# A selective-scan kernel: the softplus chain in two halves with its PSUM copies on VectorE, and the forcing term by a product with a diagonal in some states

## What is computed

```python
xs = jax.nn.silu(xs)                      # 256 tokens x 512 channels
proj = xs @ xproj_w                       # 512 columns of dt, 64 of B, 64 of C
dt = jax.nn.softplus(proj[..., :512] + dt_bias)
def step(hst, ins):                       # over the tokens
    dA = jnp.exp(dt_t[:, :, None] * A)    # 64 states per channel
    hst = hst * dA + (dt_t * x_t)[:, :, None] * B_t[:, None, :]
    y_t = jnp.einsum('bds,bs->bd', hst, C_t)
y = ys + xs * Dskip
return y * jax.nn.silu(z) @ out_w
```

## Time and profile before

| | |
|---|---|
| median of 3 runs | 3404.33 us (3403.07 to 3409.16) |
| the profiled execution's own time | 3408.53 us |
| its span, first to last instruction | 3406.7 us |
| mean granted clock of PE | 0.947 of full speed |
| steady d = 0 pass (from 985.3 us) | 197.7 us |
| steady d = 1 pass (from 1183.0 us) | 207.1 us |
| last pass (d = 1, no side work; from 3181 us) | about 185 us |
| C rows from DRAM | 1024 DMAs of 128 KB, 2.9 us to landing |

### The profile page before, as it was taken

One profiled execution on the slowest core, in us unless ns is written; L12 is line 12 of the kernel. 1 busy time (PEld: TensorE's weight loads), 2 busy tenths in 40 slices (PEclk: granted clock), 3 DMA queues, 4 the chain that ended last, 5 costly groups with the idle time before them and its releaser, 6 DMA issues.

```text
span 3406.7 us, 69419 instructions
## 1 busy us (share of the span) xinstructions
PE 3024.2 (89%) x21944; PEld 2683.9 (79%) x21944; DVE 2909.5 (85%) x3331; ACT 2989.0 (88%) x6469; POOL 2945.7 (86%) x1552
## 2 busy tenths in 40 slices
PE   8778898999988999899988999899998899998776
PEld 6568787888878888788877888788887888887765
DVE  3269998899888998889988999889988899899885
ACT  1189999899989999899999999899998999999994
POOL 0069998999888998889988998889988899899995
PEclk6689999999989999899999999899998999999998
DMA  4011111111111111111111111112111111111210
GB/s 174 0 42 43 48 45 47 42 51 48 43 48 47 47 47 42 49 45 48 45 47 43 49 48 43 48 41 52 48 43 46 48 47 46 42 45 45 54 47 26
DMA packets 163033, 162.50 MB, mean 48 GB/s; under 512 B 17610, under 2 KB 156874, under 8 KB 162644
## 3 DMA queue, kind: packets, MB, share of 16 engines
q1 hardware_dynamic: 162644, 157.69, 17.2%
HBM read 154.44 MB, written 3.18 MB: 46 GB/s over the span
## 4 chain that ended last, share of the span: by engine, by line
PE 45%; POOL 16%; ACT 15%; issue 13%; DVE 9%; DMA 1%; DVEq 1%; POOLq 0%; ACTq 0%; SPq 0%
POOL hst L408 12%; PE ps L1225 12%; PE ps L1241 11%; ACT dA L567 7%; PE ps L993 6%; ACT uBT L553 4%; DVE hst L892 4%; PE ps L1002 4%; POOL uBT L417 4%; PE ps L1065 3%; PE ps L1040 2%; PE ps L1114 1%; PE ps L1049 1%; PE ps L1233 1%; PE ps L1150 1%
## 5 line engine op out<-in xcount | busy, mean ns | idle before, releaser
L408 POOL TENSOR_TENSOR hst<-hst,C_sb 128x1024 f32<-128x1024 f32 x1024 | 2441.0, 2409 | 232.8 <-DVE hst L892 226.6
L892 DVE TENSOR_TENSOR_SCAN hst<-dA,ps 128x512 f32<-128x512 f32 x2048 | 2384.0, 1205 | 177.6 <-PE ps L1241 160.1
L567 ACT ACTIVATE dA<-dt,A 128x255 f32<-128x255 f32 x4096 | 1758.5, 504 | 2.8 <-DVE hst L892 2.7
L1225 PE MATMUL ps<-ident,uBT 128*128 128x128 f32 x8192 | 1288.2, 281 | 134.0 <-DVE hst L892 103.0
L1241 PE MATMUL ps<-ident,hst 128*128 128x128 f32 x8192 | 1267.9, 278 | 104.5 <-POOL hst L408 103.7
L1225 PEld LDWEIGHTS ps<-ident,uBT 128*128 128x128 f32 x8192 | 994.2, 145 | 299.0 <-DVE hst L892 152.5
L553 ACT ACTIVATE uBT<-uT,BT 128x512 f32<-128x512 f32 x1536 | 1052.2, 720 | 130.9 <-PE ps L1225 120.0
L1241 PEld LDWEIGHTS ps<-ident,hst 128*128 128x128 f32 x8192 | 979.6, 144 | 139.8 <-POOL hst L408 139.7
L417 POOL TENSOR_TENSOR uBT<-uT,BT 128x512 f32<-128x512 f32 x512 | 559.3, 1092 | 185.3 <-DVE uT L829 185.3
L476 ACT ACTIVATE probs<-ps,nmax 128x128 f32<-128x128 f32 (+1 forms) x256 | 93.9, 423 | 101.6 <-DVE nmax L764 100.7
L993 PE MATMUL ps<-xsT,w_xp 128*128 128x256 f32 x512 | 130.6, 380 | 0.0
(11 more groups left out here) (142 smaller groups left out, 2110.7 us busy)
## 6 DMA issues: line engine op xcount, KB each, us to landing
C_sb<-c_dram SPq DMA_DIRECT2D x1024, 128.0 KB, 2.9
gate_l<-gate_rows_dram SPq DMA_DIRECT2D x16, 256.0 KB, 3.7
x_att<-in_x_dram SPq DMA_DIRECT2D x8, 256.0 KB, 3.0
w<-in_L_cond_W_dram SPq DMA_DIRECT2D x2, 1024.0 KB
out_dram<-x_glu SPq DMA_DIRECT2D x8, 256.0 KB, 3.2
wg<-in_L_cond_mlp_w_dram SPq DMA_DIRECT2D x3, 512.0 KB, 11.4
w_xp<-_L_cond_fwd_xproj_w_dram SPq DMA_DIRECT2D x1, 1280.0 KB, 12.4
w_xp<-_L_cond_bwd_xproj_w_dram SPq DMA_DIRECT2D x1, 1280.0 KB, 15.0
```

Of the source, the lines that this page charges most:

```text
L408: pool.tensor_tensor(h, h, C_sb[:, n % FED:n % FED + 1, :].to_broadcast([P, KI, NB]), ALU.mult).then_inc(hC_ready.sem, 1)
L567: done = act.activation(dA[:, n % NT, c, lo:hi], dt[:, d, c, lo:hi], ACT.Exp, scale=A[:, d, c, n:n + 1])
L892: dve.tensor_tensor_scan(pair(hst[:, n % NR]), pair(dA[:, n % NT]), ps[:, BANK_U + (2 * n + e) % (2 * NU), :][:, way], 0.0, ALU.mult, ALU. ...
L1225: last = pe.transpose(ps[:, BANK_U + (2 * n + e) % (2 * NU), o:o + P], uBT[:, n % NF, j, c * P:(c + 1) * P], ident[:, :])
```

## The change

It has two parts. **The softplus chain** is cut into two halves `h` of 512 elements, with semaphores of their own, and DVE takes over the reading of PSUM: one add of the bias for each group (into `pre`), from which ACT makes Abs over a half in SBUF; Relu is gone, since DVE's second operation of the chain takes max(pre, 0) itself. ACT has four operations a half (Abs, Exp, 1 +, Ln), DVE four a half and a copy of half of `uT`; PE transposes u half by half. `dts` has 27 steps for 24, in other places, and their rooms change.

**The diagonal.** In the states of `BY_DIAGONAL`, ten for d = 0 and seven for d = 1, `uBT` is not u scaled by B but two 128 x 128 matrices, the identity scaled by B of that state (one for each token tile). PE multiplies `uT` by it, where it transposed before: eight matmuls in place of eight transposes. In an odd state of the list POOL makes both diagonals with one instruction of 128 x 2 x 128, and ACT makes nothing; in an even one (22, 24 and 26 of d = 0) ACT makes them with two instructions of 128 x 128.

```diff
+    BY_DIAGONAL = ((1, 3, 22, 23, 24, 25, 26, 27, 61, 63), (1, 3, 55, 57, 59, 61, 63))
+    by_pool = lambda d, n: n % 2 == 1 and n in BY_DIAGONAL[d]
+    by_act = lambda d, n: sum(not by_pool(d, k) for k in range(n))
-    STEPS = dict(... dts=24, ...)
+    STEPS = dict(... dts=27, ...)
-    dts=[HEAVY] * 12 + [LIGHT] * 2 + [HEAVY] * 3 + [LONG] + [HEAVY] * 4 + [LIGHT] * 2,
+    dts=[HEAVY] * 23 + [LIGHT, HEAVY, HEAVY, LIGHT],
-    + stage("own", "dts", 0, 2) + meanwhile(stage("own", "dts", 2, 14), stage("last", "norm", 0, 4))
-    + meanwhile(stage("own", "dts", 14, 21), stage("last", "norm", 4, 6)) + stage("own", "dts", 21, STEPS["dts"])
+    + stage("own", "dts", 0, 2) + meanwhile(stage("own", "dts", 2, 13), stage("last", "norm", 0, 4))
+    + meanwhile(stage("own", "dts", 13, 22), stage("last", "norm", 4, 6)) + stage("own", "dts", 22, STEPS["dts"])
+    half = lambda t, h: t[:, 2 * h:2 * h + 2, :]
 # POOL, forcing
-                    pool.wait_ge(uT_ready.sem, uT_ready.at(p, 1))
+                    pool.wait_ge(uT_ready.sem, uT_ready.at(p, 2))
+                if by_pool(d, n):
+                    pool.tensor_tensor(uBT[:, n % NF, :, 0:P], ident[:, :].unsqueeze(1).to_broadcast([P, TT, P]),
+                                       BT[:, d, :, n:n + 1].to_broadcast([P, TT, P]), ALU.mult).then_inc(uBT_pooled.sem, 1)
+                    return
 # ACT, prepare
-                    if i % 2 == 1 and 7 <= i < 7 + 2 * KI:
-                        act.activation(expo[:, m, :], ps[:, BANK_P + m % 2, 0:NB], ACT.Abs, bias=dtb_col[:, d, m:m + 1])
-                        act.activation(pre[:, m, :], ps[:, BANK_P + m % 2, 0:NB], ACT.Relu, bias=...).then_inc(pre_ready.sem, 1)
-                    if i == 15: Exp; if i == 16: Identity, + 1; if i == 17: Ln    (each over 128 x 1024)
+                    for h in range(2):
+                        e_h, w_h = half(expo, h), half(channels(uT[:, d]), h)
+                        if i == 10 + 4 * h:
+                            act.wait_ge(pre_ready.sem, pre_ready.at(p, 2 * h + 2))
+                            act.activation(e_h, half(pre, h), ACT.Abs).then_inc(abs_ready.sem, 1)
+                        if i == 11 + 4 * h: Exp; if i == 12 + 4 * h: Identity, + 1; if i == 13 + 4 * h: Ln
 # ACT, forcing
+                if by_pool(d, n):
+                    return
-                for j in range(TT - n % 2):
+                for j in range(TT):
+                    if n in BY_DIAGONAL[d]:
+                        done = act.activation(uBT[:, n % NF, j, 0:P], ident[:, :], ACT.Copy, scale=BT[:, d, j, n:n + 1])
+                for j in range(0 if n in BY_DIAGONAL[d] else TT - n % 2):
 # DVE, prepare
-                    if i == 17: correction; if i == 18: pre - it; if i == 19: dt; if i == 20: u; if i == 22: uT    (each over 128 x 1024)
+                    if i % 2 == 0 and 6 <= i < 6 + 2 * KI:
+                        m = (i - 6) // 2
+                        dve.wait_ge(dt_mm.sem, dt_mm.at(p, m + 1))
+                        dve.tensor_scalar(pre[:, m, :], ps[:, BANK_P + m % 2, 0:NB], dtb_col[:, d, m:m + 1], None, ALU.add).then_inc(pre_ready.sem, 1)
+                    for h in range(2):
+                        if i == 14 + 4 * h: correction; if i == 15 + 4 * h: max(x_h, 0) - it, one scalar_tensor_tensor
+                        if i == 16 + 4 * h: dt; if i == 17 + 4 * h: u    (each over 128 x 512)
+                        if i == 24 + h: uT, the half's columns, from bank BANK_P + h
 # PE, prepare
-                    if i == 21: eight transposes of u; if i == 23: wait for uT_ready
+                    if i in (22, 23): four transposes of u of half i - 22, after u_ready.at(p, h + 1); if i == 26: wait for uT_ready.at(p, 2)
 # PE, force
+                        if n in BY_DIAGONAL[d]:
+                            last = pe.matmul(to, uT[:, d, j * DI + c * P:j * DI + (c + 1) * P], uBT[:, n % NF, j, 0:P], start=True, stop=True)
+                        else:
+                            last = pe.transpose(to, uBT[:, n % NF, j, c * P:(c + 1) * P], ident[:, :])
```

More of the change, by code:

```diff
@@ L87, in order @@
             return (stage("own", "ins", 0, 10) + meanwhile(stage("last", "post"), stage("own", "ins", 10, 12))
-                    + stage("own", "dts", 0, 2) + meanwhile(stage("own", "dts", 2, 14), stage("last", "norm", 0, 4))
-                    + meanwhile(stage("own", "dts", 14, 21), stage("last", "norm", 4, 6))
-                    + stage("own", "dts", 21, STEPS["dts"]) + stage("last", "glu") + first)
+                    + stage("own", "dts", 0, 2) + meanwhile(stage("own", "dts", 2, 13), stage("last", "norm", 0, 4))
+                    + meanwhile(stage("own", "dts", 13, 22), stage("last", "norm", 4, 6))
+                    + stage("own", "dts", 22, STEPS["dts"]) + stage("last", "glu") + first)
         if not has_next:
@@ L1145, in prepare @@
                             last.then_inc(dt_mm.sem, 1)
-                    if i == 21:
-                        pe.wait_ge(u_ready.sem, u_ready.at(p, 1))
+                    if i in (22, 23):
+                        h = i - 22
+                        pe.wait_ge(u_ready.sem, u_ready.at(p, h + 1))
                         for j in range(TT):
-                            for c in range(KI):
-                                last = pe.transpose(ps[:, BANK_P + j, c * P:(c + 1) * P], pre[:, c, j * P:(j + 1) * P], ident[:, :])
+                            for c in range(2):
+                                last = pe.transpose(ps[:, BANK_P + h, j * NB + c * P:j * NB + (c + 1) * P], pre[:, 2 * h + c, j * P:(j + 1) * P], ident[:, :])
                         last.then_inc(uT_mm.sem, 1)
-                    if i == 23:
-                        pe.wait_ge(uT_ready.sem, uT_ready.at(p, 1))
+                    if i == 26:
+                        pe.wait_ge(uT_ready.sem, uT_ready.at(p, 2))
                     yield
@@ L1211, in close, with force @@
                 yield from glu(b)
-            def force(p, n, e):
+            def force(p, d, n, e):
                 r = p * NS + n
                 if e == 0:
-                    pe.wait_ge(uBT_ready.sem, uBT_ready.at(r, 1))
+                    if not by_pool(d, n):
+                        pe.wait_ge(uBT_ready.sem, uBT_ready.at(p, by_act(d, n + 1)))
                     if n % 2 == 1:
@@ L1286, in before @@
                             pe.wait_ge(pre_ready.sem, pre_ready.at(p + 1, KI))
-                        if plan.steps[j] == ("own", "dts", 21) and has_prev:
+                        if plan.steps[j] == ("own", "dts", 22) and has_prev:
                             pe.wait_ge(hT_ready[LN_GLU].sem, hT_ready[LN_GLU].at(b - 1, 1))
@@ L1315, in _ @@
             for e in range(2):
-                force(0, 0, e)
+                force(0, 0, 0, e)
             period(0, False, True)
```

83 lines of the change are left out of this document (41 added, 42 removed).

## The result

The changed kernel takes **3438.41 us**, median of 4 runs (3433.61 to 3443.28), against 3404.14 us for the kernel before (3403.07 to 3409.16): a ratio of **1.0098, 95% interval 1.008 to 1.0116**. It is slower by about 34 us, where 64 us less were forecast. The profiled execution has a span of 3437.9 us, 31.2 more than before.

The account below looks back on a forecast made before the run. No engine alone bounds: PE in product stretches, ACT then DVE in the chain, ACT at the loop edge, POOL in the last pass. -5 - 36 - 10 - 14 - 18 + 18 = -65 from 3408.5, 3340 us against the median; range 3265 to 3402.

Parts of the forecast that it names:

- item 7: PE's diagonal products, +0.9 us a state, hidden at full clock; the three more `dts` steps also cost nothing.
- item 6: DVE's new work in the chain: bias adds, split operations and contention with POOL, together +18 us (+10 to +83).
- The upper bound: DVE-POOL contention in the chain taken strictly: +2.9 us a chain, 36 us more, sum about 3375 us.
- Item 2: Softplus chain: DVE's wait for ACT vanishes, -36 us (0 to -36).
- Item 1: The first chain, which stands alone, shrinks from 11.1 to 5.9 us: -5 us.
- Item 3: Loop edge: ACT arrives relieved, so DVE waits less for `dA`: -10 us (0 to -10).
- Item 4: PE's clock recovers at the loop edge and after the d = 0 chain: -14 us, half of 28.
- Item 5: POOL's diagonal takes 0.6 us, saving 0.5 us in 37 states without POOL idle time: -18 us (0 to -30).
- Item 6's bias adds: DVE's four PSUM reads a chain lie under its waits for PE in product stretches: 0; uncovered 29 us.
- The slow rival: PE becomes the bound in diagonal states, clock below about 0.75 in states 22 to 27: some 3440 us, chance 0.10.
- DVE takes it back: Rival: uncovered bias adds (+29) and stretched DVE operations (+36) cancel the gain: 3404 to 3408 us, chance 0.09.
- the clock in one of two windows: Sign of being right: PE's clock over 0.97 around the d = 0 chain and behind the loop edge.

Follow-up runs that it names:

- e3_plan: Kernel before with only the new step list and rooms, the three added `dts` steps issuing nothing: 3448.42 us, ratio 1.0128.
- g3_after_124: Changed kernel with its side steps spread up to half state 124 in place of 120, scale 0.503: 3393.13 us, ratio 0.9963.
- e1_halves: Changed kernel with an empty list of diagonals, so the chain in halves and the new step list: 3451.92 us, ratio 1.0136.
- f3_rooms_halves: Changed kernel without diagonals and with the rooms of `dts` summing to 44 as before, in place of 52: 3435.56 us, ratio 1.0089.
- e2_diagonal: Kernel before with the diagonals alone in the change's states, old chain and old step list: 3380.59 us, ratio 0.9920.
- h3_diag_seven: Kernel before with diagonals alone, in states 1, 3, 55, 57, 59, 61, 63 of both directions: 3387.78 us, ratio 0.9937.
- f1_rooms: Changed kernel with the rooms of `dts` summing to 44 as before, in place of 52, scale 0.503: 3437.08 us, ratio 1.0103.

## Why the prediction was wrong

The forecast of 3340 us and its range of 3265 to 3402 us miss; the time came out on the slower side, which had 0.11.

**The step that failed** is in item 7: "three more steps in `dts` squeeze the scale of the rooms by a twentieth, and PE's total in those stretches is the same", costed at 0. Alone it costs 45 us, more than the 34 by which the whole is slower (e3_plan), and giving the twentieth back returns 45 (g3_after_124). That is not quite half of the miss of 98 us. At the old scale the changed kernel takes 3393.1, still 53 above the forecast; that part belongs to the items below, and no run splits it among them. I argued from PE's total, which is right: the page's PE time hardly changes between before and e3_plan (3024.2 and 3030.7 us). But the rooms don't set a total. They set how the side steps meet the states, and the kernel before stands at 0.503, just where a HEAVY step has one half state. Why a closer plan costs what it does stays open. A term that touches the place of *every* side step of fifteen passes had been given one clause; by its own rule it needed bounds from both sides.

**The second** is the contention of item 6. I took 0.5 us a chain; of my bounds the upper one (2.9) was nearly right: with the split, 51 us in 16 chains are 3.2 each, where 1.2 was put down. The evidence was in the earlier trace rows: L822, begun at 1063.19, ended 1.07 behind POOL's end at 1064.37. (The 1.2 us that the item takes off is from two of the four means; the other two, 1.21 and 1.72, add 0.5.) I read 2.25 for 1.23 as two engines that slow each other, and so as a matter of how many elements meet. It is a matter of how many *instructions* meet, so cutting four operations in two raises it. The upper bound, told beside the Trainium skill, GPSIMD Engine Reference, section 8 (Key points), with a sum of 3375 us, was the better guide: the shared interface that the page names is there, for DVE instructions with two SBUF inputs and not for the scans, as it says.

**Item 2** was right in its mechanism and not in its worth. DVE's wait for ACT went from 46.3 to 0.0 us. The text itself said that DVE is late next, with 3.8 us to win; it didn't carry the contention into that. Together the halves are worth +3.5 us on the new plan (e1_halves less e3_plan), where items 2 and 6 summed to -18, and +27 in f3_rooms_halves.

The others, one by one:

- *Item 1* (-5). From the last read of PSUM to the end of the `uT` copy the first chain takes 7.9 us (188.00 to 195.94) against 11.4 (182.72 to 194.16), 3.5 less; but PE's products of that chain began 4.2 us later in this execution (179.7 for 175.5). The first scan lies between 189.4 and 203.3 us in the kernels above, 199.5 and 190.4 in two whose code differs in one constant, so this profile can't show 5 us at this place.
- *Item 3* (-10): scans wait 9.8 us for `dA` in seven cases, 14.0 before. -4.
- *Item 4* (-14): the clock went from 0.81 to 1.00 and from 0.69 to 0.79, over the whole from 0.947 to 0.967. The clock came; its time didn't, since DVE bounds the stretch. In e2_diagonal the window is 1.1 us shorter too, but DVE's wait for ACT in the chain is down as well (27.7 us, 46.3 before, 35.6 in h3_diag_seven), so the clock's own share isn't shown. What raised it were the products (e1_halves has 0.79 there, h3_diag_seven 0.73). The last pass, mostly transposes, again has 1.00, so transposes alone don't bring it down; and the products also keep PE occupied longer, so these runs don't say whether it is their kind or their length. The Trainium skill, TensorE: Matmul & The Clock Gate, part 4 (PE-mode transpose), says that transposes don't count as busy for the clock; the window agrees with that, the last pass does not, and I had given it no chance on the last pass alone.
- *Item 5* (-18): the last pass is 3.1 us shorter where 2.5 were expected. POOL's diagonal takes 0.60 us when free and 1.06 when a DVE operation is in its way, 0.73 in the mean, for 0.6. In company the diagonals are worth 13.5 us or nothing (f1_rooms against f3_rooms_halves), alone 23. That 18 lies between is partly luck: ACT's relief, which the item left out, may be part of the 23.
- *Item 6's bias adds* (0): L829 waits 48.8 us for PE, so the adds lie under cover as said.

**The slow rival** had the size (3440) and not the mechanism. It asked for a clock below about 0.75 in the states 22 to 27; the clock is 1.00, the products take 1.16 us and DVE sets the 4.5 us a state (20 to 23). "DVE takes it back" was the rival that named the right engine; it stopped at 3404 to 3408 because it set DVE's costs against all the gains of items 1 to 5 and knew nothing of the plan.

Of the signs named beforehand, DVE's wait (0, under 10), POOL's diagonal and the last pass came out right, the clock in one of two windows (1.00 and 0.79, for 0.97). The states 20 to 25 of d = 0 at 4.1 us each in place of under 4.0 (4.2 before), the first scan 1.2 us later in place of 5 earlier, "DVE's halves at twice their free length" (1.36 and 1.22 for 0.66) and POOL's idle time, which rose where it was to fall (waits for scans 303.5 us for 226.6), showed it wrong.

## What to carry over

A change of schedule that "issues nothing" is a change: when a plan fits steps into a fixed span, three empty steps and some wider rooms cost more here than all that was gained, and the test is cheap (the old instructions under the new plan). Before cutting an operation in two to shorten a chain, look what it meets on the shared side: if the meeting costs a wait for a whole foreign instruction, twice as many operations wait more often (4 times a chain for 2.4 here), and the longer form is faster although it is later. The fastest kernels here are the kernel before with the diagonals alone (3380.59 us) and the changed one with whole-width DVE operations and the plan's end at 124 (3383.66 us, or 3383.18 with seven diagonals); the intervals of their ratios overlap.
